# A fused attention and expert kernel: the last four steps in another order, with six expert mixes added on GpSimd

## The chip, the cores and the metric

The kernel runs on one core of a Trainium2 chip. The metric is device time of one execution in microseconds (us), lower is better. The program is one launch; all five engines (TensorE or PE, VectorE or DVE, ScalarE or ACT, GpSimd or POOL, and SyncE or SP, which issues the DMAs) run their own instruction lists and meet at semaphores.

## The reference, cut to what matters

```python
x = x + tanh(g_xattn) * xattn(layernorm(x), ctx, ctx, mask, wq, wk, wv, wo)   # x: 32 x 64 x 512
x = x + tanh(g_ffn)   * ffn(layernorm(x), route_w, A, Bw)

def xattn(query, key, value, mask, ...):      # 32 query heads, 8 key/value heads, head size 128
    q, k = rope(query @ wq), rope(key @ wk);  v = value @ wv
    attn = softmax(q @ k.T / sqrt(128) + mask)          # per sequence, 64 x 64
    return (attn @ v) @ wo

def ffn(x, route_w, A, Bw):                   # 8 experts of rank 16, the best one is taken
    logits = x @ route_w.T
    weight = one_hot(argmax(logits)) * max(logits)
    return ((weight * (x @ A.T)) @ Bw.T)
```

## The kernel before, in words

The 2048 rows of x are 16 tiles of 128 rows, in two halves of 8 tiles. Keys and values of all heads are made first and kept in DRAM. Then come 64 steps (`STEPS`). A step is one group of four query heads (one key/value head) on four sequence pairs; it covers two tiles, called `bp` 0 and 1. Products in full precision are split: each f32 operand is a high part and a low part (`fp32r`), and three of the four part products are summed (`SPLIT_PRODUCTS`).

A step k goes through the engines like this:

- PE `scores(k)`: 16 matmuls into the one bank `score`; they need the rotated queries (`rope_added`) and that the scores before were read (`masked`).
- DVE `mask_scores(k)` scales, masks and finds the row maxima; GpSimd subtracts them; ACT takes the exponential; DVE `sum_rows(k)` sums and inverts; GpSimd `normalise(k)` multiplies.
- PE `turn_probs(k)` transposes into the bank `turned`; ACT `prob_high` and DVE `prob_low` split the result.
- PE `times_values(k)`: two tiles into banks `attn[0]` and `attn[1]`; ACT `attn_high` and DVE `attn_low` split it.
- PE `project_out(k, bp)`: 12 matmuls with `wo` into the same bank `attn[bp]`; DVE `add_out(k, bp)` adds the gated result to the tile's row sum `acc`. The bank is free for the next step's values only then.

The queries themselves are made beside the steps from sums of products (`product`, `q_sum`), and rotated by `q_shift` (ACT), `q_cos` (DVE), `by_sin` (GpSimd) and `q_add` (DVE). `WIDE` is 60: the steps 60 to 63 are written out by hand after the loop, since there are no more queries to make. `q_sum(31, 3)`, the last of them, is rotated there, and `scores(62)` waits for it.

When the last head group has been added to a tile, the expert part begins for it. In the second half these are tiles 8 and 9 after step 60 (lot k), 10 and 11 after step 61 (k + 1), 12 and 13 after step 62 (k + 2), 14 and 15 after step 63 (k + 3). For each tile:

- DVE `expert_norms_begin` (three small instructions), GpSimd `expert_norms` (the power -0.5), DVE `expert_norms_end` into the tile's place `expert_s` or `late_s`, two places each;
- PE "turn" (four transposes into `proj[t % 2]`) and an ACT copy;
- PE "route" (four matmuls of 136 columns into the work bank: eight logits and 128 expert features), then five DVE instructions that find the best expert and weight the features;
- PE "turn weighted" (one transpose into the same work bank) and an ACT copy;
- PE "mix" (one matmul with 512 columns, in two passes, into the work bank), and a DVE instruction that adds the gated mix to `acc`; then SP stores the tile.

Work banks before: `small` and `proj[2]` for tiles 8 to 13, `score` and `turned` for 14 and 15. The lists of PE, DVE, ACT and GpSimd are in program order; each engine takes its own list strictly in that order.

## Time and profile before

| what | value |
|---|---|
| time, median of 3 runs | 1136.95 us (1135.99 to 1137.31) |
| the profiled execution's own time | 1136.03 us |
| its span, first to last instruction | 1134.2 us |
| PE busy | 1101.8 us, 97% of the span |
| DVE busy | 900.4 us, 79% |
| ACT busy | 626.8 us, 55% |
| GpSimd busy | 611.1 us, 54% |
| mean granted TensorE clock | 0.995 of full speed |

The span is what the profile's rows cover; the rest of the execution's time (1.8 us) lies outside it. Busy PE time is summed from modelled ends of pipelined matmuls, so the pitch between the starts of two groups tells more of their cost than their busy time. PEclk is the granted clock: 1.00 is 2.4 GHz, 0.50 is 1.2 GHz.

### The profile page before, as it was taken

What the parts mean: (1) busy time and instruction counts of PE and PEld (TensorE: products, weight loads), DVE (VectorE), ACT (ScalarE), POOL (GpSimd) and SP (SyncE); (2) the same over time, 40 slices, a digit from 0 to 9 for tenths busy, and PEclk for the clock granted to TensorE, in tenths of its full rate; (3) what the DMA queues carried; (4) which work ended last, traced back from release to release, by engine and by line L of the source; (5) the groups of instructions that cost most, each with busy time, mean ns of one, the idle gap of its engine ahead of it and who ended that gap; (6) DMA issues with size and microseconds to landing.
All of it is one profiled execution on the core that took longest, in us unless ns stands there. A gap on an engine that the chain in (4) does not pass through costs nothing.

```text
span 1134.2 us, 17081 instructions
## 1 busy us (share of the span) xinstructions
PE 1101.8 (97%) x5664; PEld 921.2 (81%) x5664; DVE 900.4 (79%) x1413; ACT 626.8 (55%) x1090; POOL 611.1 (54%) x513
## 2 busy tenths in 40 slices
PE   7999999889999999999999999999999999999997
PEld 6788888678888888888888777888888888888775
DVE  7984748877787878877888999787878887877887
ACT  6462446466666666666666545455555555555441
POOL 4751458777777777777754434344434334334320
PEclk9999999989999999999999999999999999999999
DMA  6869945476464646464459745453535353542201
GB/s 226 275 233 359 341 152 210 140 280 233 149 224 150 224 148 216 159 195 181 153 214 375 236 140 163 145 183 117 196 125 191 115 179 104 175 140 75 75 1 75
DMA packets 93510, 206.27 MB, mean 182 GB/s; under 512 B 8816, under 2 KB 41712, under 8 KB 87536
## 3 DMA queue, kind: packets, MB, share of 16 engines
q1 hardware_dynamic: 93424, 205.18, 53.2%
q8 instruction: 47, 0.77, 0.3%
q14 instruction: 39, 0.32, 0.1%
HBM read 122.31 MB, written 82.84 MB: 181 GB/s over the span
## 4 chain that ended last, share of the span: by engine, by line
PE 64%; DVE 12%; POOL 11%; issue 8%; ACT 4%; DMA 0%; DVEq 0%; POOLq 0%; SPq 0%; ACTq 0%
PE attn L873 20%; PE proj L814 17%; PE score L831 7%; PE attn L766 6%; POOL rot L1624 3%; PE score L766 3%; PE turned L766 3%; POOL wq_s L1599 2%; PE turned L842 2%; PE attn L858 2%; PE attn L860 2%; DVE q_r L1102 1%; DVE q_r L1060 1%; DVE row_sum L1131 1%; DVE wo_s L1055 1%
## 5 line engine op out<-in xcount | busy, mean ns | idle before, releaser
L873 PE MATMUL attn<-wo_s,o_s 128*128 128x512 f32 x1536 | 378.5, 395 | 0.8 <-DVE o_s L1151 0.8
L814 PE MATMUL proj<-xB,wq_s 128*128 128x512 f32 x1344 | 337.2, 394 | 4.1 <-ACT copies L1422 2.2
L873 PEld LDWEIGHTS attn<-wo_s,o_s 128*128 128x128 f32 x1536 | 283.7, 188 | 58.4 <-DVE o_s L1151 1.3
L814 PEld LDWEIGHTS proj<-xB,wq_s 128*128 128x128 f32 x1344 | 253.1, 189 | 58.5 <-ACT copies L1422 2.6
L1624 POOL TENSOR_TENSOR rot<-rot,tab 128x512 f32<-128x512 f32 x112 | 169.9, 1517 | 173.3 <-ACT rot L1401 173.0
L831 PEld LDWEIGHTS score<-k_r,q_r 128*128 128x128 f32 x1024 | 123.5, 192 | 14.8 <-DVE q_r L1065 9.2
L1400 ACT ACTIVATE rot<-q_r 64x512 f32<-64x512 f32 x86 | 54.2, 630 | 144.6 <-DVE q_r L1102 139.9
L831 PE MATMUL score<-k_r,q_r 128*128 128x64 f32 x1024 | 122.9, 273 | 4.5 <-DVE q_r L1065 4.5
L1143 DVE TENSOR_TENSOR p_low<-turned,p_high 64x512 fp32r<-64x512 f32 x128 | 88.0, 688 | 42.3 <-ACT p_high L1438 40.3
L1446 ACT ACTIVATE o_s<-attn 128x512 fp32r<-128x512 f32 x128 | 69.8, 595 | 76.2 <-PE attn L860 76.1
L1065 DVE TENSOR_TENSOR q_r<-q_r,rot 128x512 f32<-128x512 f32 x86 | 89.0, 1035 | 17.1 <-POOL rot L1624 11.8
L1163 DVE SCALAR_TENSOR_TENSOR acc<-attn,gates_t,acc 128x512 f32<-128x512 f32 x128 | 95.5, 746 | 4.5 <-PE attn L873 2.5
L1624 POOL TENSOR_TENSOR rot_third<-rot_third,tab 128x512 f32<-128x512 f32 x40 | 61.5, 1538 | 68.4 <-ACT rot_third L1401 68.4
L1060 DVE TENSOR_TENSOR q_r<-q_r,tab 128x512 f32<-128x512 f32 x128 | 93.9, 734 | 4.7
L1151 DVE TENSOR_TENSOR o_s<-attn,o_s 128x512 fp32r<-128x512 f32 x128 | 81.9, 681 | 3.7 <-ACT o_s L1446 3.7
L1102 DVE TENSOR_TENSOR q_r<-copies,proj 128x512 f32<-128x512 f32 x128 | 81.7, 675 | 0.0
L1437 ACT ACTIVATE p_high<-turned 64x512 fp32r<-64x512 f32 x128 | 75.4, 589 | 9.3 <-PE turned L842 6.9
L1438 ACT ACTIVATE p_high<-turned 64x512 fp32r<-64x512 f32 x128 | 75.9, 593 | 1.5
L1422 ACT ACTIVATE copies<-proj 128x512 f32<-128x512 f32 x96 | 57.4, 598 | 27.7 <-PE proj L814 26.2
L1636 POOL TENSOR_TENSOR prob_odd<-prob_odd,row_inv 128x512 f32<-128x512 f32 x32 | 43.5, 1359 | 52.1 <-DVE row_inv L1133 52.1
L1636 POOL TENSOR_TENSOR prob_even<-prob_even,row_inv 128x512 f32<-128x512 f32 x32 | 43.1, 1348 | 47.1 <-DVE row_inv L1133 47.1
L1400 ACT ACTIVATE rot_third<-q_r 64x512 f32<-64x512 f32 x40 | 25.2, 630 | 67.7 <-DVE q_r L1102 67.2
(195 smaller groups left out, 1680.6 us busy)
## 6 DMA issues: line engine op xcount, KB each, us to landing
wq_kept<-wq_s SPq DMA_DIRECT2D x16, 1792.0 KB, 6.2
wq_s<-wq_kept SPq DMA_DIRECT2D x16, 1792.0 KB, 8.3
v_kept<-vst SPq DMA_DIRECT2D x64, 256.0 KB, 4.6
v_s<-v_kept SPq DMA_DIRECT2D x128, 128.0 KB, 4.9
wo_kept<-wo_s SPq DMA_DIRECT2D x32, 512.0 KB, 3.7
wo_s<-wo_kept SPq DMA_DIRECT2D x32, 512.0 KB, 5.1
k_kept<-kst SPq DMA_DIRECT2D x32, 256.0 KB, 2.0
wq_raw<-in_wq SPq DMA_DIRECT2D x16, 512.0 KB, 5.7
```

The source lines that it names most:

```text
L766: last = e.matmul(b[:, :], stationary, moving, start=(kt == 0 and m == 0), stop=(kt == KT - 1 and m == 2))
L814: last = e.matmul(dst[:, :], wq_s[:, b % 2, A, s, kt, :], xB[:, B, mv, kt, :], start=(first and kt == 0 and m == 0), stop=(kt == 1 and m = ...
L831: last = e.matmul(score[:, col:col + SEQ], two_heads, k_r[:, u % 2, seq * SEQ:(seq + 1) * SEQ], start=True, stop=True)
L873: last = e.matmul(attn[bp][:, :], o_s[:, s, bp, h, :], wo_s[n % WO_SLOTS][:, m, :], start=(h == 0 and i == 0), stop=(h == GROUP - 1 and i ...
L1060: e.tensor_tensor(dst, src, cos, ALU.mult).then_inc(times_cos, 1)
L1065: e.tensor_tensor(dst, dst, by_seq(rotated(r)), ALU.add).then_inc(rope_added, 1)
L1102: e.tensor_tensor(q_tile(b, j), by_seq(copies[:, copy, :]), by_seq(proj[PRODUCTS[i][2]][:, :]), ALU.add).then_inc(q_summed, 1)
L1143: e.tensor_tensor(p_low[rows, :, twin, :], turned[rows, :].rearrange("p (b n) -> p b n", b=PAIRS), p_high[rows, twin, :].bitcast(F32).rear ...
L1151: e.tensor_tensor(low, src, high.bitcast(F32), ALU.subtract).then_inc(out_low, 1)
L1163: e.scalar_tensor_tensor(out=acc[:, tile, :], in0=attn[bp][:, :], scalar=gates_t[:, 0:1], in1=acc[:, tile, :], op0=ALU.mult, op1=ALU.add). ...
L1624: e.tensor_tensor(r3, r3, sin, ALU.mult).then_inc(times_sin, 1)
L1636: e.tensor_tensor(by_row(k), by_row(k), row_inv[:, k % 2, :].unsqueeze(2).to_broadcast([P, ROWS, SEQ]), ALU.mult).then_inc(normalised, 1)
```

## The change

The diff concerns steps 60 to 63 and the expert part of tiles 8 to 15. `scores(62)` moves ahead of `times_values(60)`, and DVE takes the last query sum and the rotations earlier. Step 63 puts its values and outputs in the banks `score` and `attn[0]` (`out_bank`), and `times_values(63)` moves up to right behind `project_out(62, 1)`. Tiles 10 and 11 use `turned` and `attn[1]` as work banks, 12 and 13 `small` and `proj[2]`, 14 and 15 `score` and `attn[0]`. Tiles 12 to 15 get places of their own (`last_s`, where the inputs of the query products were), 10 and 11 the two of `late_s`. For tiles 8 to 13 the mix is no longer added by DVE: ACT reads the work bank and writes the gated mix to `mix_s` ("scale"), and GpSimd adds it to `acc` (`add_mixes`). "Turn" of tiles 12 and 13 moves ahead of `project_out(63, 1)`, and what follows on PE, ACT and DVE is ordered by single tiles rather than by lots.

```diff
--- before.py
+++ after.py
@@ -327,6 +327,9 @@
...
+        last_s = sb_at(2048, "last_s", [P, 4, DM])
+        mix_s = sb_at(2048 + 16384, "mix_s", [P, 6, DM])
@@ -398,6 +401,8 @@
...
+        mix_scaled, out_ready_g = sem("mix_scaled"), sem("out_ready_g")
@@ -475,12 +480,18 @@
         def expert_place(t):
-            return late_s[:, t % 2, :] if t >= HALF_TILES and t % 4 >= 2 else expert_s[:, t % 2, :]
+            if t >= HALF_TILES + 4:
+                return last_s[:, t - HALF_TILES - 4, :]
+            return (expert_s if t < HALF_TILES + 2 else late_s)[:, t % 2, :]
+        def out_bank(k, bp):
+            return attn[bp] if k + 1 < STEPS else (score, attn[0])[bp]
         def expert_banks(t):
...
-                work = (score, turned) if t >= TILES - 2 else (small, proj[2])
+                work = ((small, proj[2]), (turned, attn[1]), (small, proj[2]), (score, attn[0]))[(t - HALF_TILES) // 2]
@@ -612,7 +623,12 @@
             def store(n):
...
-                e.wait_ge(out_ready, n + 1)
+                if n < HALF_TILES:
+                    e.wait_ge(out_ready, n + 1)
+                elif n < TILES - 2:
+                    e.wait_ge(out_ready_g, n - HALF_TILES + 1)
+                else:
+                    e.wait_ge(out_ready, n + 1 - (HALF_TILES - 2))
@@ -852,12 +868,19 @@
...
-                    if k:
+                    if k + 1 == STEPS:
+                        if bp == 0:
+                            e.wait_ge(masked, STEPS)
+                        else:
+                            e.wait_ge(x1_added, 2 * k - 1)
+                    elif k:
...
+                    b = out_bank(k, bp)
...
-                        e.matmul(attn[bp][:, cols[twin]], v_s[:, u % 2, twin, tiles[bp], :], p_high[:, twin, cols[bp]],
+                        e.matmul(b[:, cols[twin]], v_s[:, u % 2, twin, tiles[bp], :], p_high[:, twin, cols[bp]],
...
-                    e.matmul(attn[bp][:, :], v_both[:, u % 2, tiles[bp], :], p_low[:, bp].rearrange("p t n -> p (t n)"),
+                    e.matmul(b[:, :], v_both[:, u % 2, tiles[bp], :], p_low[:, bp].rearrange("p t n -> p (t n)"),
...
             def project_out(k, bp):
@@ -870,7 +893,7 @@
...
-                        last = e.matmul(attn[bp][:, :], o_s[:, s, bp, h, :], wo_s[n % WO_SLOTS][:, m, :],
+                        last = e.matmul(out_bank(k, bp)[:, :], o_s[:, s, bp, h, :], wo_s[n % WO_SLOTS][:, m, :],
@@ -894,10 +917,16 @@
...
-                        e.wait_ge(masked, STEPS)
+                        e.wait_ge(x1_added, 2 * STEPS - TILES + t + 1)
+                    elif t >= HALF_TILES + 4:
+                        e.wait_ge(mix_scaled, t - HALF_TILES - 3)
+                    elif t >= HALF_TILES + 2:
...
+                        e.wait_ge(x1_added, 2 * (STEPS - 1))
...
-                        e.wait_ge(out_ready, t - 1)
+                        e.wait_ge(out_ready, HALF_TILES)
@@ -977,9 +1006,9 @@
             project_out(k - 1, 0)
             turn_probs(k)
             project_out(k - 1, 1)
+            scores(k + 2)
             times_values(k)
-            scores(k + 2)
             turn_probs(k + 1)
             project_out(k, 0)
             project_out(k, 1)
@@ -997,23 +1026,32 @@
             project_out(k + 2, 0)
             experts("turn weighted", k)
             project_out(k + 2, 1)
+            times_values(k + 3)
             experts("turn", k + 1)
             experts("mix", k)
-            times_values(k + 3)
             experts("route", k + 1)
             project_out(k + 3, 0)
             experts("turn weighted", k + 1)
+            experts("turn", k + 2)
             project_out(k + 3, 1)
-            experts("turn", k + 2)
-            experts("mix", k + 1)
-            experts("route", k + 2)
-            experts("turn", k + 3)
-            experts("turn weighted", k + 2)
-            experts("route", k + 3)
-            experts("mix", k + 2)
-            experts("turn weighted", k + 3)
-            experts("mix", k + 3)
+            (a0, a1), (b0, b1), (c0, c1) = (tiles_of(last) for last in range(k + 1, STEPS))
+            expert("mix", a0)
+            expert("route", b0)
+            expert("turn", c0)
+            expert("mix", a1)
+            expert("route", b1)
+            expert("turn", c1)
+            expert("turn weighted", b0)
+            expert("route", c0)
+            expert("turn weighted", b1)
+            expert("route", c1)
+            expert("mix", b0)
+            expert("turn weighted", c0)
+            expert("mix", b1)
+            expert("mix", c0)
+            expert("turn weighted", c1)
+            expert("mix", c1)
...
@@ -1145,7 +1183,7 @@
...
             def attn_low(k, bp):
-                src = attn[bp][:, :].rearrange("p (t h q) -> p h t q", t=2, h=GROUP)
+                src = out_bank(k, bp)[:, :].rearrange("p (t h q) -> p h t q", t=2, h=GROUP)
@@ -1160,7 +1198,7 @@
...
-                e.scalar_tensor_tensor(out=acc[:, tile, :], in0=attn[bp][:, :], scalar=gates_t[:, 0:1], in1=acc[:, tile, :],
+                e.scalar_tensor_tensor(out=acc[:, tile, :], in0=out_bank(k, bp)[:, :], scalar=gates_t[:, 0:1], in1=acc[:, tile, :],
...
             def expert_norms_begin(tiles):
@@ -1171,9 +1209,10 @@
             def expert_norms_end(tiles):
...
-                    if t >= HALF_TILES + 2:
-                        e.wait_ge(mixed, t - 3)
-                    elif t >= 2:
+                    if t >= HALF_TILES + 4:
+                        e.wait_ge(produced, BLOCKS * Q_BLOCKS)
+                    elif t >= 2 and t < HALF_TILES + 2:
@@ -1283,20 +1322,21 @@
...
+            before = ropes_of(k - 1)[1][0]
             mask_scores(k)
             attn_low(k - 1, 0)
             attn_low(k - 1, 1)
+            q_sum(*q)
             sum_rows(k)
-            q_sum(*q)
             mask_scores(k + 1)
+            q_cos(*before)
+            q_add(*before)
...
+            q_cos(*q)
             prob_low(k, 0)
-            q_cos(*ropes_of(k - 1)[1][0])
+            q_add(*q)
             prob_low(k, 1)
...
-            q_add(*ropes_of(k - 1)[1][0])
-            q_cos(*q)
-            q_add(*q)
             sum_rows(k + 1)
             attn_low(k, 0)
@@ -1320,27 +1360,31 @@
             attn_low(k + 2, 0)
             attn_low(k + 2, 1)
-            expert_norms_begin(tiles_of(k + 1))
+            expert_norms_begin(tiles_of(k + 1)[:1])
             prob_low(k + 3, 0, 1)
+            expert_norms_begin(tiles_of(k + 1)[1:])
+            add_out(k + 2, 0)
...
-            add_out(k + 2, 0)
...
-            experts("mix", k)
             attn_low(k + 3, 0)
             attn_low(k + 3, 1)
...
             experts("route", k + 1)
...
-            for bp in range(PAIRS):
-                add_out(k + 3, bp)
-                expert_norms_begin(tiles_of(k + 3)[bp:bp + 1])
-            expert_norms_end(tiles_of(k + 3))
-            experts("mix", k + 1)
-            experts("route", k + 2)
-            experts("route", k + 3)
-            experts("mix", k + 2)
-            experts("mix", k + 3)
+            (b0, b1), (c0, c1) = tiles_of(k + 2), tiles_of(k + 3)
+            add_out(k + 3, 0)
+            expert_norms_begin([c0])
+            expert_norms_end([c0])
+            add_out(k + 3, 1)
+            expert_norms_begin([c1])
+            expert("route", b0)
+            expert_norms_end([c1])
+            expert("route", b1)
+            expert("route", c0)
+            expert("route", c1)
+            expert("mix", c0)
+            expert("mix", c1)
...
@@ -1441,7 +1485,7 @@
...
-                src = attn[bp][:, :].rearrange("p (t h q) -> p h t q", t=2, h=GROUP)
+                src = out_bank(k, bp)[:, :].rearrange("p (t h q) -> p h t q", t=2, h=GROUP)
@@ -1454,6 +1498,9 @@
...
+                elif what == "scale" and t < TILES - 2:
+                    e.wait_ge(mixed, t + 1)
+                    e.activation(mix_s[:, t - HALF_TILES, :], b_work[:, :], ACT.Copy, scale=gates_t[:, 1:2]).then_inc(mix_scaled, 1)
             def between(k, at):
@@ -1547,15 +1594,24 @@
             attn_high(k + 2, 1)
...
             experts("turn weighted", k)
-            experts("turn", k + 1)
             attn_high(k + 3, 0)
             attn_high(k + 3, 1)
+            experts("turn", k + 1)
+            experts("scale", k)
             experts("turn weighted", k + 1)
             experts("turn", k + 2)
-            experts("turn", k + 3)
-            experts("turn weighted", k + 2)
-            experts("turn weighted", k + 3)
+            (a0, a1), (b0, b1), (c0, c1) = (tiles_of(last) for last in range(k + 1, STEPS))
+            expert("scale", a0)
+            expert("turn", c0)
+            expert("scale", a1)
+            expert("turn", c1)
+            expert("turn weighted", b0)
+            expert("turn weighted", b1)
+            expert("scale", b0)
+            expert("turn weighted", c0)
+            expert("scale", b1)
+            expert("turn weighted", c1)
...
@@ -1708,6 +1764,12 @@
...
+            def add_mixes(k):
+                for t in tiles_of(k):
+                    here = acc[:, t % HALF_TILES, :]
+                    e.wait_ge(mix_scaled, t - HALF_TILES + 1)
+                    e.tensor_tensor(here, here, mix_s[:, t - HALF_TILES, :], ALU.add).then_inc(out_ready_g, 1)
@@ -1719,8 +1781,12 @@
...
-            for last in range(k + 1, STEPS):
-                expert_norms(last)
+            expert_norms(k + 1)
+            expert_norms(k + 2)
+            add_mixes(k)
+            expert_norms(k + 3)
+            add_mixes(k + 1)
+            add_mixes(k + 2)
```

## Rows read from the trace of the kernel before

**Rows 1.** Windows: us, then busy time and instructions by engine, PEclk, DMA share, GB/s

```profile
1061.43:1084.96 23.53, 20.98 (x106) 17.13 (x106) 18.63 (x31) 10.77 (x18) 7.81 (x8) 0.93 0.23 79
...
1109.19:1134.20 25.01, 18.19 (x93) 12.55 (x91) 17.77 (x54) 3.62 (x10) 2.44 (x4) 0.98 0.17 64
```

**Rows 2.** Chain that ended last: start us, us, what

```profile
1046.94 1.73 PE score L831 x16
...
1052.40 2.72 PE attn L873 x12
...
1074.02 2.50 PE score L831 x16
1076.52 0.85 PE turned L842 x4
1077.38 6.17 PE attn L873 x24
```

**Rows 3.** Windows of two us ahead of the clock's fall and in it

```profile
1072.00:1074.00 2.00, 0.73 (x3) 0.41 (x3) 1.90 (x4) 1.19 (x2) 0.00 (x0) 1.00 0.18 68
...
1076.00:1078.00 2.00, 2.00 (x9) 1.84 (x9) 1.38 (x2) 0.59 (x1) 0.00 (x0) 0.50 0.00 0
```

**Rows 4.** Timeline of DVE: start us, us, what [idle before it <- releaser]

```profile
1064.70 0.69 DVE L1131 TENSOR_REDUCE row_sum<-prob_even 128x8 f32<-128x512 f32 x1 [0.62 <-ACT prob_even L1430]
...
1065.54 0.68 DVE L1102 TENSOR_TENSOR q_r<-copies,proj 128x512 f32<-128x512 f32 x1
1066.13 0.68 DVE L1124 SCALAR_TENSOR_TENSOR prob_odd<-score,mask_sb 128x512 f32<-128x512 f32 x1
...
1068.91 0.68 DVE L1143 TENSOR_TENSOR p_low<-turned,p_high 64x512 fp32r<-64x512 f32 x1 [0.72 <-ACT p_high L1438]
...
1071.22 0.75 DVE L1163 SCALAR_TENSOR_TENSOR acc<-attn,gates_t,acc 128x512 f32<-128x512 f32 x1
1071.89 0.68 DVE L1065 TENSOR_TENSOR q_r<-q_r,rot_third 128x512 f32<-128x512 f32 x1
...
1073.28 0.69 DVE L1065 TENSOR_TENSOR q_r<-q_r,rot 128x512 f32<-128x512 f32 x1
...
1094.92 0.17 DVE L1188 TENSOR_REDUCE top<-small 128x1 f32<-128x8 f32 x1 [0.18 <-PE small L904]
...
1096.12 0.15 DVE L1188 TENSOR_REDUCE top<-proj 128x1 f32<-128x8 f32 x1
...
1131.00 0.75 DVE L1204 SCALAR_TENSOR_TENSOR acc<-turned,gates_t,acc 128x512 f32<-128x512 f32 x1
```

**Rows 5.** Timeline of GpSimd in steps 60 and 61

```profile
1068.62 1.30 POOL L1624 TENSOR_TENSOR rot<-rot,tab 128x512 f32<-128x512 f32 x1
1074.88 1.04 POOL L1636 TENSOR_TENSOR prob_odd<-prob_odd,row_inv 128x512 f32<-128x512 f32 x1 [4.97 <-DVE row_inv L1133]
```

**Rows 6.** Timeline of PE in steps 62 and 63 and the experts behind

```profile
1104.78 1.02 PE L917 MATMUL small<-lora_bT,expert_s 128*128 128x512 f32 x2
1105.64 1.02 PE L917 MATMUL proj<-lora_bT,expert_s 128*128 128x512 f32 x2
...
1107.43 1.09 PE L904 MATMUL small<-routedT,late_s 128*128 128x136 f32 x8
...
1109.19 2.98 PE L873 MATMUL attn<-wo_s,o_s 128*128 128x512 f32 x12
...
1120.87 1.17 PE L904 MATMUL small<-routedT,expert_s 128*128 128x136 f32 x8 [1.67 <-DVE acc L1204]
...
1128.97 1.12 PE L917 MATMUL score<-lora_bT,late_s 128*128 128x512 f32 x2 [0.24 <-ACT late_s L1456]
```

**Rows 7.** Timeline of ACT in the experts of tiles 12 to 15

```profile
1117.08 1.09 ACT L1453 ACTIVATE expert_s<-proj 128x512 f32<-128x512 f32 x2 [2.91 <-PE proj L738]
```

**Rows 8.** Groups of GpSimd by line and form

```profile
L1624 POOL TENSOR_TENSOR rot<-rot,tab 128x512 f32<-128x512 f32 x112 | 169.9, 1517 | 173.3 <-ACT rot L1401 173.0
```

**Rows 9.** One line's instructions: duration ns min/median/max

```profile
L1035 DVE TENSOR_SCALAR expert_s<-acc,moments,rstd x12: 537/542/1276, 639.0 to 1113.8; 128x512 f32<-128x512 f32 x12
```

## The prediction

> **What bounds the kernel now.** I read the page first: PE is busy for 97% of the span, so only what keeps PE waiting, or slows its clock, can give time back. The windows by stage say where that is. Up to 1061 us the loop over steps runs unchanged code. The reader is to compare busy PE with the length of the other stretches [rows 1]: from 1061.43 to 1084.96 PE has work for 20.98 of 23.53 us at a granted clock of 0.93, and from 1109.19 to the end for 18.19 of 25.01 us. The 24 us between them hold one gap of 0.84 us. So there are two places to win, with different causes.
>
> *First place, steps 60 and 61.* The chain of waits shows `scores(62)` start at 1074.02, when `q_add(31, 3)` ends on DVE (1073.28 + 0.69 [rows 4]). PE waited 1.27 us for it, and 0.87 us earlier for the low probabilities. In the two us before, PE was busy for 0.73; behind that the granted clock falls to 0.50, which is 1.2 GHz [rows 3]. The same groups cost more there: 16 score matmuls 2.50 instead of 1.73, four transposes 0.85 instead of 0.43 (half), 24 output matmuls 6.17 instead of 2 x 2.72 = 5.44 [rows 2]. That is 0.77 + 0.42 + 0.73 = 1.9 us lost to the clock.
>
> *Second place, the experts of the last tiles.* PE's timeline behind 1109.19 has gaps of 0.17, 0.85, 1.67, 0.64 and 0.24 us, of which two stand in the rows [rows 6]: "route" of tile 12 waits 1.67 us for DVE's addition of a mix, the last mix matmul but one 0.24 us for an ACT copy. They are 3.6 us by the modelled ends, and each hides a drain besides; so I don't add gaps but sum pitches.
>
> **The change, first place.** DVE, in order. Before, from `mask_scores(61)` at 1066.13 to the start of `q_add(31, 3)` at 1073.28 there are 7.15 us. The new list has the same instructions in between but for one `prob_low` (0.68, 0.7 with its issue), one `add_out` (0.67, from 1071.22 to 1071.89), and the 0.72 us wait for the high probabilities, which now falls behind other work [rows 4]: 7.15 - 0.7 - 0.67 - 0.72 = 5.06 us. The list also starts earlier: `q_sum(31, 3)` slips into the 0.62 us for which DVE waits ahead of `sum_rows(60)`, at no cost, and `mask_scores(61)` starts at 1065.54. `q_add` starts at 1065.54 + 5.06 = 1070.6 and ends at 1071.3. GpSimd's sine product began at 1068.62, behind a subtraction that now comes 0.6 earlier, and takes 1.30 [rows 5]: done by 1069.9 at the latest, no limit.
>
> PE ends `project_out(59, 1)` at 1070.4 as before and starts `scores(62)` at 1071.3 instead of 1074.02; behind it come the values of step 60. Their price: between scores and outputs of an ordinary step, 1052.40 - 1046.94 - 1.73 = 3.73 us, lie 12 product matmuls of the same shape as 12 output matmuls (2.72) and two tiles' values [rows 2], so 1.0 us. PE is through at 1074.0. What is queued behind the moved scores: values, `turn_probs(61)` and the outputs of step 60, on PE alone; no DMA moves here. `turn_probs(61)` needs the normalised rows. Before, `sum_rows(61)` came right behind `q_add`, and `normalise(61)` started 1074.88 - 1073.28 = 1.60 us after it and took 1.04 [rows 4, 5]; now `prob_low` and `add_out` stand between, so it starts at 1070.6 + 1.60 + 0.7 + 0.67 = 1073.6 and ends at 1074.6, 1.3 us earlier. Transposes 0.43, outputs 5.44: PE reaches 1080.5 where it was at 1083.55. **3.0 us**, of which 1.9 is the clock if it stays up. It does if PE has work for 2.7 of the 4.2 us that were mostly empty. The opposite bound is 1.1 us, if it falls all the same. The two waits left (0.9 and 0.6 us) are the new limit, both for DVE.
>
> From there to `project_out(62, 1)` PE's list is the same, and the waits in it (for `add_out(60, 1)`, for `o_s` of step 62) hang on the same DVE chain, which is shifted with it: 0. Moving `times_values(63)` up by itself gives 0 too: the same turns, mixes, values and routes stand between 1103.91 and 1109.19 in either order, and PE has no gap there [rows 6]. What it buys is earlier `o_s` of step 63 (ACT at about 1104.7, DVE at 1105.2 to 1106.5), so that DVE is free for norms and routing of tiles 12 and 10. All this is relative to the old clock; the 3.0 us come off afterwards.
>
> **The change, second place.** PE's work behind 1109.19 is the same in both kernels. Pitches from [rows 2, 6]: "turn" has four transposes as the probabilities have, 0.43; "turn weighted" a quarter, 0.11; "mix" 1105.64 - 1104.78 = 0.86; two "routes" 1109.19 - 1107.43 = 1.76, so 0.88; outputs 2.72. Sum: 2 x 2.72 + 4 x 0.43 + 6 x 0.11 + 6 x 0.86 + 4 x 0.88 = 16.5 us. Without a wait PE ends at 1125.7.
>
> Which waits remain? Routing costs DVE 1096.12 - 1094.92 = 1.20 us a tile [rows 4]. Tiles 10 and 11 are routed by 1110.9, norms of 12 and 13 end at 1112.0, as the outputs of tile 0 of step 63 do: "turn" of 12 and 13 fits between the outputs. These end at 1115.8 (16.5's part so far). Then, one tile each: mix 10 and route 12 to 1117.5, turn 14 (its norm was done at 1115.1), mix 11, route 13 to 1119.7, turn 15. For that last one DVE does `add_out` and norm statistics of tile 15 (from 1115.9, 1.8 us), routes tile 12 (1.20) and ends the norm (0.54): 1119.5. PE asks at 1119.7, so it holds by 0.2 us. Routes of 13, 14 and 15 follow each other on DVE every 1.2 us, and PE's list asks for them 1.1 to 1.9 us apart. ACT now has a "scale" for six tiles; its nearest row is a copy of the same 128 x 512, 1.09/2 = 0.55 [rows 7]. `scale(12)` stands ahead of the small copy of tile 14, 0.1 us late; `scale(13)` stands ahead of that of tile 15, whose transpose ends at the same time, so the last mix waits for drain, copy and hand-over, 0.55 us. I add 0.3 us for the narrow places (DVE before turn 15, and turn 12). Sum of waits 0.95; the last mix in its own modelled length 1.12 instead of 0.86, 0.26 more [rows 6]. PE ends at 1125.7 + 0.95 + 0.26 = 1126.9, DVE's last addition (0.75 [rows 4]) at 1127.7 instead of 1131.75: **4.0 us**.
>
> GpSimd's additions aren't in the trace. Below, the nearest is an addition of 1.04 us with one full operand [rows 5]; above, the sine product, 1.52 in the mean [rows 8]. I take 1.3. Each has cover: the ones of tiles 8 and 9 run from 1109.1 to 1111.7, ahead of the power for tile 14 (1113.9). Those of 12 and 13 start when `scale(12)` ends, at 1123.95, and end by 1126.6; stores go in order on SP, that of tile 13 ahead of 14 and 15, and the last store waits for DVE at 1127.7 anyway. So 0. The store itself is moved, not changed: 1134.20 - 1131.75 = 2.45 us behind the last addition.
>
> A rule that speaks against it: the Trainium skill, GPSIMD Engine Reference, section Specifications, says that GpSimd shares its SBUF interfaces with VectorE and contends with VectorE's two-port modes and with two SBUF inputs. The row on the norm's last instruction agrees as far as it goes: 0.54 us in the median, 1.28 at most [rows 9]. By the rule three of these (tiles 12, 13, 15) would meet additions and DVE would lose up to 2 us, the third of them on the path.
>
> **Sum.** 3.0 + 4.0 = 7.0 us of the profiled span, 1127.2, so 1129.0 for the profiled execution (1136.03). The median of the runs is 0.9 above that execution, so 1136.95 - 7.0 = 1129.9 us. The case's own range: waits of 0.5 to 1.9 us instead of 0.95 in the second place, and 2.7 to 3.3 us in the first, so 1129.2 to 1131.2.
>
> **Rivals.**
> - *The clock falls all the same.* PE still waits twice near 1071 and 1074 us. Against it: PE has 2.7 us of work between them. Price 1.9: 1131.8 us. 14%.
> - *The single tiles don't mesh.* The additions on GpSimd stretch DVE's norm ends from 0.54 to 1.28 [rows 9], turn 12 and turn 15 are late by 0.5 and 0.7 us, each routing behind is too, and the last copies on ACT wait another turn: 2 us of the 4.0 come back as waits. 1131.9 us. For it: the margin of 0.2 us; against it: DVE has six additions fewer. 15%.
> - *DVE is the bound and nothing is won.* DVE is busy for 18.63 and 17.77 us of the two stretches [rows 1]; if its dependent instructions can't be packed, gaps only change places: 1136.9. Against it: five of the gaps wait for something that was only queued badly. 3%.
> - *Slower: GpSimd's additions set the end.* Each us over the 1.8 us at which the last one ends with DVE (1123.95 + 2 x 1.8) costs 2 us. To be slower than before by over 0.2% they must take over 6 us each. At 7: 1129.9 + 2 x 5.2 = 1140.3. Nothing in the rows is near. 2%.
>
> **How the numbers follow.** The forecast has 66%. With the first two rivals it is 95%, which is "faster"; 0.2% (2.3 us) is about what a measurement of this kernel can tell from no change. The range runs from 1128.4, where every wait in the second place but the last is gone and `q_add` is earlier by its 0.3, to 1132.6, which takes in both first rivals and not both at once. Faster 0.94, same 0.04, slower 0.02.
>
> **What would show it.** After: `scores(62)` ahead of the values of step 60, at about 1071.3; granted clock 1.00 from 1074 to 1080; `project_out(60, 1)` ending near 1080.5. `project_out(63, 0)` starting near 1106.2. PE busy for 17.5 of the last 21 us, "turn" of tile 15 with hardly a wait, the last mix with one of about 0.5 us. GpSimd's additions at 1.0 to 1.5 us and the last before DVE's last. It is wrong if `sum_rows(61)` starts later than 1073 (1072.6 by the steps above), if the clock row shows 0.50 again, or if a norm's end beside an addition is the releaser of PE.

## The result, and the profile after

The changed kernel takes 1134.35 us (median of 13 runs, 1131.36 to 1135.59) against 1137.77 us (13 runs) before: ratio 0.9972 with the interval 0.9965 to 0.9979, so 3.2 us faster. Forecast were 7.0 us, 1129.9 us and the range 1128.4 to 1132.6. The direction was right, the size was not, and the time lies outside the range. The kernel before took 0.8 us more here than in the three runs from which the forecast started; a range moved up by that would end at 1133.4 and would still miss the time.

The profiled execution has a span of 1132.6 us against 1134.2. To compare two profiles the span has to be cut, because the unchanged part ahead of step 60 differs by 0.8 us between these two executions (`turn_probs(60)` starts at 1067.05 before, at 1067.89 after), and by up to 2.3 us among the profiles of this study (1066.25 to 1068.55), which all share that part. The timeline of PE after:

```profile
1067.89 0.60 PE L858 MATMUL turned<-tab,prob_even 128*128 128x128 f32 x4
...
1072.81 2.58 PE L847 MATMUL score<-k_r,q_r 128*128 128x64 f32 x16 [1.55 <-DVE q_r L1103]
...
1077.00 0.83 PE L858 MATMUL turned<-tab,prob_odd 128*128 128x128 f32 x4
1077.76 5.76 PE L896 MATMUL attn<-wo_s,o_s 128*128 128x512 f32 x24
...
1086.68 0.61 PE L858 MATMUL turned<-tab,prob_even 128*128 128x128 f32 x4
...
1109.19 3.00 PE L896 MATMUL score<-wo_s,o_s 128*128 128x512 f32 x12
...
1121.87 0.66 PE L754 MATMUL proj<-tab,last_s 128*128 128x128 f32 x4 [1.48 <-DVE last_s L1073]
...
1128.00 1.13 PE L946 MATMUL attn<-lora_bT,last_s 128*128 128x512 f32 x2 [0.37 <-ACT last_s L1500]
```

From `turn_probs(60)` to `turn_probs(62)` it took 1086.68 - 1067.89 = 18.79 us; before it was 1086.69 - 1067.05 = 19.64, so 0.85 us came of the first place, where 3.0 were forecast. From the start of `project_out(63, 0)` to the end of DVE's last addition it took 1129.17 + 0.75 - 1109.19 = 20.73 us; before 1131.75 - 1109.19 = 22.56 [rows 4, 6], so 1.83 us of the second place instead of 4.0. The last store took 0.23 us more (spans are printed to a tenth, so this is good to about 0.1). Between the two places nothing moved: 22.51 and 22.50 us. The sum 0.85 + 1.83 - 0.23 less the 0.84 of the unchanged part is the 1.6 us between the spans. The windows (us, busy by engine, PEclk, DMA share, GB/s):

```profile
1074.00:1076.00 2.00, 2.00 (x11) 2.00 (x11) 1.06 (x3) 0.00 (x0) 0.82 (x1) 0.51 0.01 2
1076.00:1078.00 2.00, 2.00 (x9) 1.55 (x9) 0.82 (x2) 1.33 (x3) 0.22 (x1) 0.63 0.00 0
...
1062.14:1084.95 22.81, 21.12 (x109) 17.27 (x109) 19.56 (x31) 10.78 (x18) 8.80 (x8) 0.93 0.25 81
...
1109.19:1132.60 23.41, 18.01 (x93) 12.56 (x91) 15.62 (x41) 6.37 (x14) 8.53 (x8) 0.99 0.23 90
```

The first place still has a PEclk of about 0.5 (1.2 GHz), earlier than in the kernel before [rows 3], and 0.93 in the mean of the stretch, as before [rows 1]: `scores(62)` took 2.58 us, the 24 output matmuls 5.76. In the second place PE is busy for 18.0 of 23.4 us. GpSimd is now busy for 8.53 us there, where it was 2.44 [rows 1].

DVE's timeline and GpSimd's, in both places:

```profile
1067.72 0.68 DVE L1098 TENSOR_TENSOR q_r<-q_r,tab 128x512 f32<-128x512 f32 x1
1068.51 1.35 DVE L1103 TENSOR_TENSOR q_r<-q_r,rot_third 128x512 f32<-128x512 f32 x1
1069.78 0.74 DVE L1201 SCALAR_TENSOR_TENSOR acc<-attn,gates_t,acc 128x512 f32<-128x512 f32 x1
1070.44 1.12 DVE L1098 TENSOR_TENSOR q_r<-q_r,tab 128x512 f32<-128x512 f32 x1
...
1072.09 0.67 DVE L1103 TENSOR_TENSOR q_r<-q_r,rot 128x512 f32<-128x512 f32 x1
...
1074.18 0.67 DVE L1169 TENSOR_REDUCE row_sum<-prob_odd 128x8 f32<-128x512 f32 x1
...
1109.22 1.21 DVE L1234 TENSOR_SCALAR top<-top 128x8 f32<-128x8 f32 x1
...
1111.11 0.16 DVE L1232 TENSOR_REDUCE top<-top 128x1 f32<-128x8 f32 x1
...
1118.87 1.32 DVE L1234 TENSOR_SCALAR top<-top 128x8 f32<-128x8 f32 x1
...
1120.43 1.38 DVE L1073 TENSOR_SCALAR last_s<-acc,moments,rstd 128x512 f32<-128x512 f32 x1
...
1129.17 0.75 DVE L1243 SCALAR_TENSOR_TENSOR acc<-attn,gates_t,acc 128x512 f32<-128x512 f32 x1 [0.85 <-PE attn L946]
```

```profile
1067.88 1.42 POOL L1687 TENSOR_TENSOR prob_odd<-prob_odd,neg_max 128x512 f32<-128x512 f32 x1 [0.28 <-DVE neg_max L1165]
1069.27 1.75 POOL L1680 TENSOR_TENSOR rot<-rot,tab 128x512 f32<-128x512 f32 x1
...
1109.10 2.54 POOL L1771 TENSOR_TENSOR acc<-acc,mix_s 128x512 f32<-128x512 f32 x2
...
1118.90 2.63 POOL L1771 TENSOR_TENSOR acc<-acc,mix_s 128x512 f32<-128x512 f32 x2
1126.26 2.49 POOL L1771 TENSOR_TENSOR acc<-acc,mix_s 128x512 f32<-128x512 f32 x2 [4.73 <-ACT mix_s L1503]
```

The reader is to set the two side by side. DVE's cosine product and addition take 0.68 us when alone; here the addition at 1068.51 takes 1.35 and the product at 1070.44 takes 1.12, both beside GpSimd, and GpSimd's two take 1.42 and 1.75 instead of 1.04 and 1.30 [rows 5]. `add_out` at 1069.78, between them and also beside GpSimd, takes its usual 0.74: it reads PSUM (the banks lie there, `acc` and the `*_s` places in SBUF). At 1118.87 an instruction on eight columns takes 1.32 us; its usual is 0.29. It ends at 1120.19, about where the first of GpSimd's two additions ends (half of 2.63 us behind 1118.90). The norm's end of tile 15 behind it takes 1.38 instead of 0.55, and PE waits 1.48 us for it. Not every instruction from SBUF to SBUF is held: the `TENSOR_REDUCE` on the same eight columns at 1111.11 takes its usual 0.16 beside the additions of tiles 8 and 9 (1109.10 to 1111.64), while the `TENSOR_SCALAR` at 1109.22 takes 1.21 beside them.

The three things by which the prediction said it would be known as wrong have all come: `sum_rows(61)` starts at 1074.18 (1073.3 if the 0.84 us of the unchanged part are taken off) and not before 1073, the clock row shows 0.51, and a norm's end beside an addition releases PE.

### The profile page after: what moved, and what is told of

Read it like the earlier page. It is cut to its first block, busy times and chain, and to the rows that moved or that the text cites. A ratio compares the mean times of both kernels' runs of the same rounds, so it can differ in the third digit from the quotient of the medians.

```text
span 1132.6 us, 17085 instructions
## 1 busy us (share of the span) xinstructions
PE 1103.6 (97%) x5664; PEld 923.1 (82%) x5664; DVE 899.3 (79%) x1407; ACT 630.8 (56%) x1096; POOL 619.2 (55%) x519
## 4 chain that ended last, share of the span: by engine, by line
PE 64%; DVE 14%; POOL 10%; issue 7%; ACT 4%; DMA 0%; DVEq 0%; SPq 0%; ACTq 0%; POOLq 0%
PE attn L896 20%; PE proj L830 17%; PE score L847 7%; PE attn L782 6%; POOL rot L1680 4%; PE score L782 3%; PE turned L782 3%; POOL wq_s L1655 2%; PE attn L881 2%; PE turned L858 2%; PE attn L883 2%; DVE q_r L1140 2%; DVE q_r L1098 1%; DVE row_sum L1169 1%; DVE wo_s L1093 1%
## 5 line engine op out<-in xcount | busy, mean ns | idle before, releaser
L896 PE MATMUL attn<-wo_s,o_s 128*128 128x512 f32 x1524 | 374.6, 395 | 0.8 <-DVE o_s L1189 0.8
```

The lines of the kernel that those rows point to most:

```text
L896: last = e.matmul(out_bank(k, bp)[:, :], o_s[:, s, bp, h, :], wo_s[n % WO_SLOTS][:, m, :], start=(h == 0 and i == 0), stop=(h == GROUP - 1 ...
```

## The experiments

Two lengths are compared, since they hold still between executions while the rest of the span drifts: **X**, from the start of `turn_probs(60)` to that of `turn_probs(62)`, and **Y**, from the start of `project_out(63, 0)` to the end of DVE's last instruction. S is what remains to the end of the span; it is good to 0.05 us, as spans are printed to a tenth. Each ratio is to runs of the kernel before made beside that kernel, whose median was 1136.40 us for e1 to e4, 1137.38 for e5 to e8 and 1137.78 for e9 to e11. Medians of different groups are therefore compared by their ratios.

| kernel | median us (runs) | ratio to before, interval | X, lowest PEclk of its 2 us windows | Y | S |
|---|---|---|---|---|---|
| before | 1137.77 (13) | | 19.64, 0.50 | 22.56 | 2.45 |
| changed | 1134.35 (13) | 0.9972 (0.9965 to 0.9979) | 18.79, 0.51 | 20.73 | 2.68 |
| e1 first place only | 1134.99 (12) | 0.9987 (0.9977 to 0.9997) | 17.77, 1.00 | 22.60 | 2.50 |
| e2 second place only | 1135.24 (12) | 0.9986 (0.9977 to 0.9996) | 19.86, 0.50 | 20.73 | 2.63 |
| e3 no additions on GpSimd | 1130.58 (6) | 0.9953 (0.9936 to 0.9969) | 17.74, 1.00 | 18.81 | 2.45 |
| e4 filler | 1132.70 (6) | 0.9961 (0.9949 to 0.9974) | 17.73, 1.00 | 20.72 | 2.60 |
| e5 sine first | 1134.46 (9) | 0.9974 (0.9964 to 0.9984) | 19.44, 0.54 | 20.72 | 2.59 |
| e6 mixes of 10, 11 on DVE | 1133.04 (5) | 0.9966 (0.9953 to 0.9979) | 20.20, 0.50 | 19.16 | 2.66 |
| e7 ranks in PSUM | 1131.56 (5) | 0.9955 (0.9943 to 0.9968) | 17.73, 1.00 | 19.01 | 2.66 |
| e8 e5 and e6 and tail order | 1132.52 (5) | 0.9964 (0.9951 to 0.9976) | 19.39, 0.52 | 18.41 | 3.38 |
| e9 tail kept clear | 1130.73 (5) | 0.9942 (0.9928 to 0.9956) | 20.19, 0.50 | 17.99 | 2.53 |
| e10 e9 and filler | 1129.58 (5) | 0.9925 (0.9911 to 0.9938) | 17.74, 1.00 | 17.94 | 2.47 |
| e11 before and filler | 1134.65 (6) | 0.9974 (0.9962 to 0.9985) | 18.24, 1.00 | 22.57 | 2.51 |

**e1_first_only**: the kernel before with PE's `scores(62)` moved and DVE's list of steps 60 and 61, as in the diff ahead.

> The kernel before with the first place of the change alone: scores(62) ahead of the values of step 60, and DVE's new order of query sum and rotations. The prediction had 3.0 us for it. Theory A (the place is worth little, since DVE and GpSimd slow each other around the last rotation, PE still waits about 1.5 us in one piece and the clock still falls): 0.5 to 1 us faster than before, ratio 0.9992 to 0.9997, and PEclk 0.5 somewhere from 1073 to 1079 us in the profile. Rival B (the place gives what was forecast, and the profiled execution of the changed kernel was an unlucky one): 3 us faster, ratio 0.9974.

```profile
1066.82 0.60 PE L842 MATMUL turned<-tab,prob_even 128*128 128x128 f32 x4
...
1071.74 2.00 PE L831 MATMUL score<-k_r,q_r 128*128 128x64 f32 x16 [1.55 <-DVE q_r L1066]
...
1075.20 0.66 PE L842 MATMUL turned<-tab,prob_odd 128*128 128x128 f32 x4 [0.47 <-POOL prob_odd L1638]
...
1084.59 0.61 PE L842 MATMUL turned<-tab,prob_even 128*128 128x128 f32 x4
```

Ratio 0.9987, between the two theories' numbers. The profile has no low clock in steps 60 and 61, and X is 1084.59 - 1066.82 = 17.77 us, 1.9 shorter than before. With the same order of instructions X is 18.79 in the changed kernel's profile. So theory A's "the clock still falls" isn't true of each execution.

**e2_second_only**: the changed kernel with those two lists as before.

> The changed kernel with the first place undone: the order of steps 60 and 61 is that of before, on PE and DVE. Theory A: 1.8 to 2.7 us faster than before, ratio 0.9977 to 0.9984, nearly all of the change's gain, and turn of tile 15 waits 1.5 us on PE. Rival B (the second place gives little, the gain of the changed kernel in its median comes from the first): ratio above 0.999.

Y is 20.73, the same as in the changed kernel, and PE waits 1.48 us for turn 15 again. In the medians each place alone is worth about 1.5 us, and the two are additive within the intervals. Theory A was right on the wait and on Y, but the second place is about half of the change's gain in the median, not nearly all of it. Rival B is out by Y, which is 1.83 us shorter than before; the ratio alone (0.9977 to 0.9996) would leave a little room for it.

**e3_no_adds**: this leaves out the mixes of tiles 8 to 13.

```diff
-                    e.tensor_tensor(here, here, mix_s[:, t - HALF_TILES, :], ALU.add).then_inc(out_ready_g, 1)
+                    e.tensor_tensor(small_g[:, t - HALF_TILES:t - HALF_TILES + 1], power[:, :], power[:, :], ALU.add).then_inc(out_ready_g, 1)
```

> The changed kernel without GpSimd's six 512-column additions: a one-column addition of constants stands in for each, so the mixes of tiles 8 to 13 are left out of the output. Theory A (the additions block DVE's tensor_scalar instructions): the routing's tensor_scalar that took 1.2 and 1.3 us for 8 columns is back at 0.29, the norm's end of tile 15 at 0.55, PE doesn't wait for turn 15, and the kernel is 1.5 to 1.9 us faster than the changed one, ratio to before 0.9955 to 0.9958. Rival B (these durations come from the order of the single tiles or from bank conflicts, not from GpSimd): they stay, and the time is within 0.3 us of the changed kernel's.

DVE's timeline, the same two instructions and its last:

```profile
1116.78 0.29 DVE L1235 TENSOR_SCALAR top<-top 128x8 f32<-128x8 f32 x1
...
1117.31 0.54 DVE L1074 TENSOR_SCALAR last_s<-acc,moments,rstd 128x512 f32<-128x512 f32 x1
...
1125.50 0.75 DVE L1244 SCALAR_TENSOR_TENSOR acc<-attn,gates_t,acc 128x512 f32<-128x512 f32 x1 [0.85 <-PE attn L947]
```

0.29 and 0.54 us instead of 1.32 and 1.38, no wait for turn 15, Y 18.81 instead of 20.73: GpSimd's additions cost 1.9 us of the second place. Theory A holds. Counted from `project_out(63, 0)`, and against this kernel, `project_out(63, 1)` starts 0.3 us later in the changed kernel and turn 15 another 1.7 us later. So the additions of tiles 8 and 9 cost a little too, by the routing of tile 10 ahead of turn 12 (1.21 us for its eight columns).

**e4_filler**: six matmuls whose result nobody reads, where PE waits.

```diff
+            for _ in range(6):
+                e.matmul(small[:, :], wq_s[:, (Q_BLOCKS - 1) % 2, B22, 0, 0, :], xB[:, B22, 0, 0, :], start=True, stop=True)
             scores(k + 2)
```

> The changed kernel with six more matmuls (128x512, into the idle bank small, result unused) ahead of scores(62), 1.4 us of work where PE waits 1.55 us for q_add. Theory A (what is lost in the first place is mostly the clock, which falls since PE is idle there): PEclk stays 1.00 from 1070 to 1082 us, the score matmuls take 1.73 us, and the kernel is 1.5 to 1.9 us faster than the changed one in executions in which the clock fell, 1 to 1.9 in the median, ratio to before 0.9955 to 0.9963, though it does more work. Rival B (the clock follows something else, or its loss is hidden behind DVE): no faster, or slower by up to 0.2 us.

```profile
1070.15 1.52 PE L1010 MATMUL small<-xB,wq_s 128*128 128x512 f32 x6
1071.83 2.00 PE L847 MATMUL score<-k_r,q_r 128*128 128x64 f32 x16 [0.16 <-DVE q_r L1105]
```

The clock is 1.00 in all of steps 60 and 61, `scores(62)` takes 2.00 us by its busy time (2.58 after), X is 17.73. The median is 1.2 us under the changed kernel's by the ratios, as theory A had it, but the intervals overlap, and one profile with a high clock proves little, since e1 and e3 have it without filler. The single runs say more. The mean granted clock of a run is 0.992 in 4 of 13 of the changed kernel, 4 of 12 of e1, 2 of 6 of e3, 2 of 5 of e6, 2 of 5 of e9 and none of 5 of e7. These are the slowest of e1 (1136.9 to 1137.6 against 1133.8 to 1135.4) and of e3 (1133.1 and 1133.6 against 1130.2 to 1130.6); in the changed kernel they are among the slowest (1135.1 to 1135.6), with two others at 0.997 (1134.9 and 1135.1). No run of the three kernels with filler (e4, e10, e11; 17 runs) is at 0.992. The mean of a whole run is a coarse sign, since each profile has other stretches of low clock too, one of them between 200 and 260 us. The comparison that isolates the filler with a clear interval is e11.

**e5_sin_first**:

```diff
+            by_sin(ROPE_NO["q", Q_BLOCKS - 1, 3])
             subtract_max(k + 1)
-            by_sin(ROPE_NO["q", Q_BLOCKS - 1, 3])
...
             q_add(*before)
-            add_out(k - 1, 0)
             q_cos(*q)
-            prob_low(k, 0)
             q_add(*q)
-            prob_low(k, 1)
-            add_out(k - 1, 1)
+            prob_low(k, 0, 1)
             sum_rows(k + 1)
+            add_out(k - 1, 0)
+            add_out(k - 1, 1)
```

> The changed kernel with another order in the first place alone: GpSimd takes the sine product of q(31, 3) ahead of the subtraction for step 61, and DVE takes both rotations first, then the low probabilities and sum_rows(61), then both add_outs of step 59. Theory A (the first place gave no more than the clock since q_add(31, 3) and sum_rows(61) stood behind work that nobody waited for yet, and behind GpSimd): scores(62) starts within 0.3 us of project_out(59, 1)'s end, turn_probs(61) 1.2 us earlier against turn_probs(60) than in the changed kernel at full clock, PEclk stays 1.00, and the kernel is 1.2 to 2.4 us faster than the changed one, ratio to before 0.995 to 0.996. Rival B (DVE and GpSimd only get in each other's way elsewhere): scores(62) starts earlier, but turn_probs(61) less than 0.4 us earlier.

DVE and PE:

```profile
1068.39 1.68 DVE L1098 TENSOR_TENSOR q_r<-q_r,tab 128x512 f32<-128x512 f32 x1
1070.17 1.35 DVE L1103 TENSOR_TENSOR q_r<-q_r,rot_third 128x512 f32<-128x512 f32 x1
...
1072.22 0.69 DVE L1103 TENSOR_TENSOR q_r<-q_r,rot 128x512 f32<-128x512 f32 x1
```

```profile
1072.97 2.00 PE L847 MATMUL score<-k_r,q_r 128*128 128x64 f32 x16 [1.04 <-DVE q_r L1103]
1076.11 0.50 PE L881 MATMUL attn<-p_high,v_s 128*128 128x256 f32 x2 [1.15 <-DVE acc L1201]
```

A miss. Putting the rotations one behind the other on DVE put them wholly beside GpSimd: 1.68 and 1.35 us for two instructions of 0.68. `scores(62)` starts 4.42 us behind `turn_probs(60)` instead of 4.92, but PE then waits 1.15 us more for `add_out`, the clock falls, and X is 19.44. The gain from the earlier row sum is eaten by the later values. Neither the 1.2 us of theory A nor a high clock came; rival B had the earlier `scores(62)` and the missing gain.

**e6_dve_mixes**: "scale" and `add_mixes` for tiles 8, 9, 12 and 13 only, and on DVE

```diff
             expert("route", c1)
+            experts("mix", k + 1)
             expert("mix", c0)
```

> The changed kernel with the mixes of tiles 10 and 11 added by DVE again, from their own banks, behind the last routing, where DVE was idle for 1.5 us; GpSimd keeps those of 8, 9, 12 and 13. All outputs are the reference's. Theory A (only the two additions that run beside route 12 and the norm of tile 15 cost anything): PE doesn't wait for turn 15, 1.5 us faster than the changed kernel, the same as without any addition, ratio to before 0.995 to 0.9965. Rival B (DVE's two more additions push the last two back): 0.5 us or less.

Y is 19.16, 1.6 less than in the changed kernel, with every mix still added and no wait for turn 15: the mechanism of theory A. It isn't quite the same as without any addition: 0.35 us remain against e3, as the additions of tiles 8 and 9 still hold the routing of tile 10 (1.21 us). Of the median only 0.7 us is seen by the ratios (0.9966 against 0.9972, intervals overlap); two of the five runs are at a mean clock of 0.992, the profiled one among them, whose X is 20.20.

**e7_ranks_psum**:

```diff
                 logits = b[:, 0:EXPERTS]
+                if t >= HALF_TILES:
+                    ranks = b[:, ROUTED:ROUTED + EXPERTS]
```

> The changed kernel with the eight rank values of the routing written to and read from the work bank in PSUM instead of SBUF, in tiles 8 to 15. Theory A (GpSimd's additions hold back those DVE instructions that read SBUF in the fast form or read two SBUF operands, however small they are, and not those that read PSUM): the routing's tensor_scalar of tile 12 takes about 0.3 us instead of 1.32 beside the same addition, while the norm's end of tile 15 is still slowed; turn 15 waits 0.5 to 1.0 us less, 0.5 to 1 us faster than the changed kernel. Rival B (any DVE instruction is held back beside GpSimd, or the wait is for the result to be written): it still takes over 1 us.

DVE and GpSimd at the same place:

```profile
1116.67 0.28 DVE L1236 TENSOR_SCALAR top<-small,top 128x8 f32<-128x8 f32 x1
...
1117.20 1.04 DVE L1073 TENSOR_SCALAR last_s<-acc,moments,rstd 128x512 f32<-128x512 f32 x1
```

```profile
1116.69 2.68 POOL L1773 TENSOR_TENSOR acc<-acc,mix_s 128x512 f32<-128x512 f32 x2
```

The same instruction beside the same addition takes 0.28 instead of 1.32 when its eight values come from PSUM. The norm's end, SBUF to SBUF, is still held: 1.04. Y falls by 1.7, more than I gave it, since the earlier end of the routing also moves the norm's end, and PE hardly waits for turn 15. (The routing of tile 10 is back at 0.28 too, so this covers more than one instruction.) By the ratios it is 1.9 us in the median, with intervals that just overlap. VectorE as a whole isn't held beside GpSimd, so rival B is out: it depends on the form of the instruction and on where it reads.

**e8_all**: e5, e6 and

```diff
             expert("mix", b1)
-            expert("mix", c0)
             expert("turn weighted", c1)
+            expert("mix", c0)
```

and on ACT the copy of turn weighted of tile 15 ahead of the gated copy of tile 13.

> The orders of the two kernels above that move the first place and the mixes of tiles 10 and 11, together, and in the tail turn weighted of tile 15 ahead of mix 14 on PE and its copy ahead of the gated copy of tile 13 on ACT. Theory A: the gains add, 1.2 to 2.4, 1.5 and 0.5 us: 3.2 to 4.4 us faster than the changed kernel, ratio to before 0.993 to 0.994. Rival B (at the end DVE's row of routings and additions is the bound, so the gains of the tail don't add): 2.5 to 3 us faster than the changed one.

Y 18.41, but S 3.38. DVE's last instruction and GpSimd's last two additions:

```profile
1126.57 0.75 DVE L1243 SCALAR_TENSOR_TENSOR acc<-attn,gates_t,acc 128x512 f32<-128x512 f32 x1
```

```profile
1124.40 2.51 POOL L1771 TENSOR_TENSOR acc<-acc,mix_s 128x512 f32<-128x512 f32 x2 [5.76 <-ACT mix_s L1503]
```

GpSimd ends its last addition at 1126.91, DVE its own at 1127.32. The stores go out in order in one queue, so those of tiles 13, 14 and 15 become free within 0.4 us of each other. By the ratios the median is 0.9 us under the changed kernel's, where theory A had at least 3.2 and rival B at least 2.5: neither size came. Rival B was right that the gains don't add, and wrong on where. Y + S is 21.79, no better than e6's 21.82, and X is 19.39 with a low clock, as in the other profile of e5's order.

**e9_tail**: ranks in PSUM, the order of e8's tail, and

```diff
-            add_mixes(k + 1)
-            add_mixes(k + 2)
+            e.wait_ge(ln_done, NORM_NO["expert", TILES - 1] + 1)
+            add_mixes(k + 1)
...
             expert("route", c1)
+            experts("mix", k + 2)
             expert("mix", c0)
```

with "scale" for tiles 8 to 11 only.

> The changed kernel with a tail in which DVE and GpSimd keep clear of each other: rank values in PSUM; GpSimd adds the mixes of tiles 8 to 11, those of 10 and 11 only after the norm of tile 15 has ended; DVE adds those of 12 to 15 at the end, where it was idle; turn weighted of tile 15 ahead of mix 14. Theory A: from the start of project_out(63, 0) to the end of the span 20.9 us (changed kernel 23.4, before 25.0), so about 2.5 us faster than the changed kernel, ratio to before 0.995. Rival B (the last stores, now four close together, cost what the additions did): no more than 1.7 us faster than the changed kernel.

Y + S is 20.52 us against 23.41 in the changed kernel and 25.01 before: theory A (20.9). The median gains 3.4 us on the changed kernel by the ratios, and the intervals don't overlap. Rival B is out, S is 2.53 with four stores of DVE's tiles close together. The windows of the profiled execution show the low clock at its worst:

```profile
1072.00:1074.00 2.00, 1.13 (x9) 1.13 (x10) 1.94 (x4) 0.00 (x0) 0.00 (x0) 0.93 0.70 234
1074.00:1076.00 2.00, 2.00 (x11) 2.00 (x11) 1.12 (x3) 0.00 (x0) 0.77 (x1) 0.50 0.06 23
...
1078.00:1080.00 2.00, 2.00 (x7) 1.55 (x6) 1.80 (x4) 1.71 (x4) 0.00 (x0) 0.50 0.00 0
```

**e10_tail_filler**: that with e4's filler.

> The kernel above with the six unused matmuls ahead of scores(62) as well. Theory A: PEclk 1.00 through steps 60 and 61 in the profile, 17.7 us from turn_probs(60) to turn_probs(62), and another 0.5 to 1.2 us in the median over the kernel above, since that one's clock falls in a part of its executions; ratio to before 0.9940 to 0.9950, the fastest of all. Rival B (the clock doesn't matter in the median): within 0.3 us of the kernel above.

X 17.74, Y 17.94, S 2.47; DVE's last instruction:

```profile
1125.78 0.75 DVE L1247 SCALAR_TENSOR_TENSOR acc<-attn,gates_t,acc 128x512 f32<-128x512 f32 x1
```

1129.58 us, ratio 0.9925 (0.9911 to 0.9938): 8.5 us faster than before, the fastest of all, and beyond theory A's ratios. Its median is 1.15 us under that of e9, measured beside it, which is for theory A, but the interval overlaps that of e9 a little.

**e11_before_filler**: three such matmuls ahead of `times_values(60)` and five ahead of `scores(62)` in the kernel before.

> The kernel before with eight unused matmuls in its two waits of steps 60 and 61, three ahead of the values of step 60 and five ahead of scores(62); nothing else differs. Theory A (most of what the first place was worth is the clock, not the order of instructions): PEclk stays 1.00, turn_probs(60) to turn_probs(62) takes 18.3 us instead of 19.6, 1.3 us faster than before, ratio 0.9988, against 17.7 us with the new order. Rival B (the order is what counts): under 0.4 us faster than before.

```profile
1066.25 0.60 PE L842 MATMUL turned<-tab,prob_even 128*128 128x128 f32 x4
...
1071.82 1.30 PE L985 MATMUL small<-xB,wq_s 128*128 128x512 f32 x5
1073.24 2.00 PE L831 MATMUL score<-k_r,q_r 128*128 128x64 f32 x16
1075.20 0.66 PE L842 MATMUL turned<-tab,prob_odd 128*128 128x128 f32 x4
...
1084.49 0.61 PE L842 MATMUL turned<-tab,prob_even 128*128 128x128 f32 x4
```

```profile
1074.10 1.04 POOL L1640 TENSOR_TENSOR prob_odd<-prob_odd,row_inv 128x512 f32<-128x512 f32 x1 [4.97 <-DVE row_inv L1137]
```

X = 1084.49 - 1066.25 = 18.24 us at full clock, with the order of before. It was 19.64 with the fall of the clock. The waits are as long as before (6.99 us from `turn_probs(60)` to `scores(62)`); they are only filled. Theory A had this. The median is 3.0 us down by the ratio (1.7 to 4.3), more than X explains: 1.4 us, or 1.6 against e2, which has the same order and a low clock. Other executions of before than the profiled one may lose more there, as e6 and e9 do in the new order (2.5 us). The single runs fit that: of the ten runs of before beside e11, five have a mean clock of 0.992 and take 1138.1 to 1138.9 us, the other five have 0.994 and take 1136.4 to 1137.4, while the six of e11 have 0.995 or 0.997 and take 1133.9 to 1135.7. No profile shows where in the span those slower runs lose it.

## Why the prediction was wrong, step by step

**The bounds.** That the two places were where time could be won, and that nothing between them would move, held (22.50 and 22.51 us). That moving `times_values(63)` up by itself gives 0 fits this: no time went there.

**First place, 3.0 us forecast, 0.85 measured in the profile.** The missing 2.15 us are 0.6 of the order, 0.5 of the clock's price and 1.05 of a clock that fell all the same.

- *The order, 1.1 us forecast, 0.50 measured* (18.24 in e11 against 17.74 in e10, both at full clock). The step was "`q_add` starts at 1065.54 + 5.06 = 1070.6": it summed DVE's pitches from a stretch in which these instructions ran almost free of GpSimd. In the new order `q_add(31, 2)` meets the subtraction and `q_cos(31, 3)` the sine product. They took 1.35 and 1.12 instead of 0.69 each, 1.1 us more. Relative to `turn_probs(60)`, `scores(62)` came at 4.92 us where 4.25 were forecast. The trace before had a sign of it that the sum passed over: the one rotation that ran beside the end of the sine product [rows 5] took 0.94 us.

```profile
1069.52 0.94 DVE L1060 TENSOR_TENSOR q_r<-q_r,tab 128x512 f32<-128x512 f32 x1
```

- *The clock's price, 1.9 us forecast, 1.40 measured* (19.64 before, 18.24 in e11, the same order). The step was the sum 0.77 + 0.42 + 0.73: it counted the longer score matmuls in full. At full clock PE would have waited there anyway: in e11 GpSimd ends `normalise(61)` at 1074.10 + 1.04 = 1075.14, and the transposes start at 1075.20. They start only 0.3 us earlier, against `turn_probs(60)`, than in the kernel before (8.95 us and 9.27).
- *The clock stays up.* "It does if PE has work for 2.7 of the 4.2 us" was a judgement, and the outcome it forecast came in half of the profiles. Six were taken with the order of the change in steps 60 and 61 and no filler: e1, e3 and e7 show no fall and X of 17.7 to 17.8, the changed kernel 18.79, e6 20.20 and e9 20.19. PE's one wait ahead of `scores(62)` is the same in all six, 1.54 to 1.57 us. What decides between them isn't shown by these profiles; it stays open. That the fall costs the 1.0 to 2.5 us is shown by X and by the pitches at 0.50, and by the filler in the kernel before (e11), which takes the fall and 1.4 us of X away. That single runs with a mean clock of 0.992 are those that fell longest is argued from e6 and e9 alone.

**Second place, 4.0 us forecast, 1.83 measured.** The sum of pitches and the waits of PE and ACT were nearly right: without GpSimd's additions the place gives 22.56 - 18.81 = 3.75 us (e3), and the last mix waits as forecast (0.52 us by its start, 0.55 forecast). The step that failed is "Each has cover [...] So 0" for the additions, which cost 1.92 us. Their length was right (1.25 to 1.3 us each). The cover was worked out for tiles 8 and 9 and for 12 and 13; for 10 and 11 no place was worked out, and these two, from 1118.90 to 1121.53, cost most of it. What I priced was whether somebody waits for the additions, not whom they hold back while they run.

The second rival had this mechanism at 15%. Its total, 2 us, is right, its parts are not, so the closeness is in part luck: it had turn 12 late by 0.5 us, turn 15 by 0.7 and the rest in the last copies, and measured are 0.3, 1.7 and nothing. The row on which it rested [rows 9] was read as a rare maximum. In the trace before it was the time in five of the 12 places, each time for the second of two tiles, which started while GpSimd was at a subtraction (the first of these at 639.45 us, beside one from 639.16 to 640.43); the others took 0.54. The eight-column instruction gave the same sign, which the prediction did not use: it took 0.60 to 0.62 us in four of its 16 places, each beside a sine product, and 0.29 in the others.

```profile
L1195 DVE TENSOR_SCALAR top<-top x16: 290/291/616, 648.0 to 1127.7; 128x8 f32<-128x8 f32 x16
```

In the tail it became 1.32 us, and since DVE's margin ahead of turn 15 was 0.2 us, nearly all of that became PE's wait.

**The rule that spoke against it.** The Trainium skill, GPSIMD Engine Reference, section Specifications, names two forms that contend with GpSimd: VectorE's two-port modes and two SBUF inputs. The traces agree for the second: `q_add` and `q_cos` took 1.35 and 1.12 us instead of 0.69. For the first they agree if the two `TENSOR_SCALAR` instructions, the norm's end (1.38 instead of 0.55) and the small one of the routing (1.32 instead of 0.29), run in such a mode, which no row here names. The instructions with one input in PSUM (0.74) and the `TENSOR_REDUCE` (0.16) were spared. I cited the rule and gave its price of up to 2 us a chance of 15%; with it the sum would have been 5 us.

**The store.** 2.45 us were taken over, 2.68 came. With two of the last additions on GpSimd the stores of tiles 12 to 15 leave closer together; e3, without them, has 2.45, e8, with the closest, 3.38. In e9, with four stores of DVE's tiles within 2.5 us, it is 2.53. That it is the closeness is argued from these, not isolated.

**The chances.** Both first rivals came true together, 1.9 us in the tail and 1.05 us of the clock in the profile, and the range had excluded just that ("not both at once"). A range that takes in both ends at 1129.9 + 1.9 + 2.0 = 1133.8. The rest, 0.6 us of the order, 0.5 of the clock's price, 0.25 of the pitches in the second place and 0.2 of the store, stood in no rival.

## What to carry to other kernels

Before work is moved to GpSimd, list which VectorE instructions will run beside it: here the `TENSOR_SCALAR` instructions from SBUF to SBUF and the `TENSOR_TENSOR` ones with two operands in SBUF were held back, even at eight columns, and those that read an operand in PSUM weren't, nor was `TENSOR_REDUCE`. Keeping the eight rank values of each tile in PSUM was worth 1.7 us of Y here, about as much as taking two of six additions away (1.6). Where TensorE waits, a few unused matmuls into an idle bank can be worth as much as a better order, since the clock stayed up in every profile with them (in the medians 3.0 us for the kernel before, interval 1.7 to 4.3; the new order alone 1.5, interval 0.3 to 2.6). Compare two executions by stretches that begin and end on the same instructions, since the rest of a long span drifts by more than such a change is worth.

## What the runs showed of the hardware that was not expected

- A VectorE instruction on 128x8 f32 in SBUF took 1.32 us beside a GpSimd addition of 128x512 and 0.29 without one; with its input in PSUM it took 0.28 beside the same addition. A `TENSOR_REDUCE` on the same eight columns in SBUF took 0.16 with and without an addition beside it. GpSimd pays too: its subtraction takes 1.42 to 1.50 us beside such VectorE instructions and 1.04 alone, its sine product 1.75 and 1.28. Which of the two pays differs: in the loop over the steps of the kernel before, the cosine product keeps its 0.69 us in the median while the sine product, which runs beside it, takes 1.52 in the mean [rows 8].
- GpSimd's full additions took 1.24 to 1.34 us each, near the 1.3 that was interpolated.
- The same instructions of steps 60 and 61, with the same wait of PE of 1.54 to 1.57 us, run through at 2.4 GHz in three profiles and fall to 1.2 GHz in three others. In the changed kernel's profile two windows of 2 us in a row are below full clock, in those of e6 and e9 at least four, and X is longer accordingly (18.79 against 20.2).
